# Attention stages: where the exponential, its maximum and the transposes' copy run

## The reference

```python
def _L1_attn_ref(x, w_qkv, b_qkv, w_out, b_out):
    ...
    q, k = _rope(q, k)
    scores = jnp.einsum('bhtd,bhsd->bhts', q, k) / jnp.sqrt(jnp.float32(Dh))
    scores = jnp.where(causal, scores, -jnp.inf)
    probs = jax.nn.softmax(scores, axis=-1)
    out = jnp.einsum('bhts,bhsd->bhtd', probs, v)
    ...
x = _layernorm(x + _L1_attn_ref(x, ...), axis=-1)
```

| stage | time in the span, us | scores from | mask | output projection |
|---|---|---|---|---|
| L1_attn | 5119 to 5480 | x, with rotary embedding | causal | yes |
| L1_xattn | 5480 to 5800 | x and the context | one per batch element | yes |
| L2_xattn ("recalled") | 6534 to 6790 | x and one remembered key and value for all heads | none | yes |
| L3_self | 7110 to 7430 | x, gain and shift in its norm | causal | no |
| L3_cross | 7430 to 7700 | Y and the context, gain and shift | none | no |

## Time and profile before

### The profile page before, as it was taken

How to read it: one execution, slowest core, us unless ns; L and a number is a source line. 1 busy time by engine, 2 the same in 40 slices (tenths; PEclk the granted TensorE clock), 3 DMA queues, 4 the chain that set the end, 5 groups by cost and what they waited for, 6 DMA issues and landing times. The chain is left out here.

```text
span 8333.2 us, 92849 instructions
## 1 busy us (share of the span) xinstructions
PE 6721.0 (81%) x34116; PEld 4705.7 (56%) x34116; DVE 3959.2 (48%) x8807; ACT 1842.1 (22%) x2726; POOL 1376.6 (17%) x1101
## 2 busy tenths in 40 slices
PE   5889888888888888898599998876476766778698
PEld 3666665666666566666456665554243543555454
DVE  7454455654445565444300003545487344554444
ACT  2222122222222222221121211222211233223111
POOL 2221122222212222221200001312000100222100
PEclk8776677676666767766799999877655777778899
DMA  0000000000000000000000000000000000000000
GB/s 26 1 1 1 1 1 1 1 1 1 1 1 1 1 1 1 1 1 14 35 11 21 21 11 6 0 25 13 2 1 8 20 4 4 3 17 6 4 17 23
DMA packets 13607, 64.63 MB, mean 8 GB/s; under 512 B 1168, under 2 KB 5648, under 8 KB 11152
## 3 DMA queue, kind: packets, MB, share of 16 engines
q1 hardware_dynamic: 13200, 59.09, 2.0%
HBM read 56.99 MB, written 2.10 MB: 7 GB/s over the span
## 5 line engine op out<-in xcount | busy, mean ns | idle before, releaser
L806 PE MATMUL psum<-arena,weights 32*32 32x64 f32 x8192 | 860.4, 287 | 0.0
L773 PE MATMUL psum<-arena 128*128 128x256 f32 x2048 | 596.8, 443 | 319.3 <-DVE arena L979 312.6
L806 PEld LDWEIGHTS psum<-arena,weights 32*32 32x32 f32 x8192 | 763.5, 152 | 5.8
L1219 PE MATMUL psum<-arena 128*128 128x512 f32 x1600 | 711.7, 599 | 59.5 <-DVE Y L1283 35.8
L773 PEld LDWEIGHTS psum<-arena 128*128 128x128 f32 x2048 | 448.3, 224 | 526.1 <-issue 349.5
L796 PEld LDWEIGHTS psum<-arena 32*32 32x32 f32 (+2 forms) x6144 | 591.0, 157 | 256.6 <-issue 253.9
L796 PE MATMUL psum<-arena 32*32 32x64 f32 (+2 forms) x6144 | 670.3, 293 | 0.0
L1231 PE MATMUL psum<-arena 128*128 128x256 f32 x2624 | 583.0, 380 | 4.1 <-DVE arena L1324 4.1
L1300 DVE SCALAR_TENSOR_TENSOR Y<-psum,arena,Y 128x256 f32<-128x256 f32 x416 | 172.5, 478 | 849.0 <-PE psum L1231 849.0
L1231 PEld LDWEIGHTS psum<-arena 128*128 128x128 f32 x2624 | 499.1, 190 | 111.7 <-issue 43.5
L144 POOL TENSOR_TENSOR arena<-arena,eps 128x4 f32<-128x4 f32 (+2 forms) x76 | 15.1, 199 | 3221.9 <-DVE arena L139 3221.9
(11 more groups left out here) (418 smaller groups left out, 10541.0 us busy)
## 6 DMA issues: line engine op xcount, KB each, us to landing
arena<-in_experts_L_ffn SPq DMA_DIRECT2D x8, 2052.0 KB, 8.2
arena<-in_ctxT SPq DMA_DIRECT2D x16, 512.0 KB, 3.5
arena<-in_experts_L_ffn SPq DMA_DIRECT2D x18, 384.0 KB, 3.0
weights<-in_w_L_ffn SPq DMA_DIRECT2D x1, 3072.0 KB, 9.8
weights<-in_w_L_attn SPq DMA_DIRECT2D x1, 3024.5 KB, 13.1
weights<-in_w_L_ffn SPq DMA_DIRECT2D x1, 2753.0 KB, 12.8
weights<-in_w_L_relu SPq DMA_DIRECT2D x1, 2436.0 KB, 9.4
X<-in_x SPq DMA_DIRECT2D x1, 2048.0 KB, 8.3
```

Of the source, the lines that this page charges most:

```text
L773: mm = nc.tensor.matmul(ps[:, 2 + 2 * hh + m // 2, (m % 2) * 2 * P:(m % 2 + 1) * 2 * P], kz[:, p % 2, hh, m, :], kq[:, p % 2, m, :, :], st ...
L806: mm = nc.tensor.matmul(ps[rows, 4 + h, m * DK:(m + 1) * DK], Tt[rows, h * M + m, :], rhs, start=True, stop=True)
L1219: mm = nc.tensor.matmul(ps[:, bank, :], W[s][name][:, c, f * P:(f + 1) * P], xT[:, g, c, :], start=(c == 0), stop=(c == C - 1))
```

## The change

In `attention_stage` alone:

- The scale 1/4 moves into the constant `w.heads`, so the scores come out of TensorE already scaled. With a mask VectorE only adds it.
- VectorE takes the maximum with its sign turned (`negate=True`) and no longer subtracts; the semaphore `maxima_ready` stands for `shifted`.
- ScalarE computes the exponential head by head: 8 activations of 128x128 per unit, each with its head's negated maximum as a bias per partition. It reads `pr` with a mask and PSUM without.
- The copy of the transposes to `pT` goes from ScalarE to VectorE, where it stands behind the passes of the next unit and ahead of the normalisation.
- Without a mask, TensorE's scores wait for the exponentials (`probs_ready`) of the unit whose PSUM they overwrite, as does VectorE's maximum for its `mx` buffer; ScalarE waits for the transposes of the unit whose `pr` it overwrites.

```diff
...
@@ -396,7 +396,7 @@
                         if not recalled:
                             pe.wait_ge(v_ready, (g + 1) * 2)
                     if j >= 2:
-                        pe.wait_ge(shifted, g * UNITS + j - 1)
+                        pe.wait_ge(maxima_ready if mask else probs_ready, g * UNITS + j - 1)
                     out = s_psum(j)
                     for b in range(2):
                         mm = nc.tensor.matmul(out[:, b * 4:b * 4 + 4, :], qT[:, c, u * P:(u + 1) * P],
@@ -485,13 +486,15 @@
 
             def units(g, more):
                 for j in STEPS:
-                    if 1 <= j <= UNITS:
-                        act.wait_ge(probs_turned, g * UNITS + j)
-                        nc.scalar.copy(pT[:, (j - 1) % 2, :, :], pt_psum).then_inc(probsT_ready, 1)
                     if j < UNITS:
-                        act.wait_ge(shifted, g * UNITS + j + 1)
-                        nc.scalar.activation(pr[:, j % 2, :, :], pr[:, j % 2, :, :], ACT.Exp,
-                                             scale=1.0 if mask else DH ** -0.5).then_inc(probs_ready, 1)
+                        act.wait_ge(maxima_ready, g * UNITS + j + 1)
+                        if j >= 2 and not mask:
+                            act.wait_ge(probs_turned, g * UNITS + j - 1)
+                        frm = pr[:, j % 2, :, :] if mask else s_psum(j)
+                        for h in range(HH):
+                            a = nc.scalar.activation(pr[:, j % 2, h, :], frm[:, h, :], ACT.Exp,
+                                                     bias=mx[:, j % 2, h:h + 1])
+                        a.then_inc(probs_ready, 1)
                     if more and j == UNITS + 1:
                         copy_x(g + 1)
                     if out_proj and j >= 3 and j % 2 == 1 and (j - 3) // 2 < TILES:
@@ -532,21 +535,25 @@
                     if j < UNITS:
                         n = g * UNITS + j
                         dve.wait_ge(scores_ready, n + 1)
-                        if j >= 2:
-                            dve.wait_ge(probs_turned, n - 1)
-                        s = s_psum(j)
+                        scores = s_psum(j)
                         if mask:
+                            if j >= 2:
+                                dve.wait_ge(probs_turned, n - 1)
                             if mask == "batch":
                                 if j == 0:
                                     dve.wait_ge(mask_loaded, (g + 1) * 16)
                                 m = mk[:, j // C, :]
                             else:
                                 m = w.causal
-                            chain(dve.scalar_tensor_tensor(out=pr[:, j % 2, :, :], in0=s, scalar=DH ** -0.5,
-                                                           in1=bc(m, 1, HH), op0=ALU.mult, op1=ALU.add))
-                            s = pr[:, j % 2, :, :]
-                        chain(dve.tensor_reduce(mx[:, j % 2, :], s, AX.X, ALU.max))
-                        dve.tensor_tensor(pr[:, j % 2, :, :], s, bc(mx[:, j % 2, :], 2, P), ALU.subtract).then_inc(shifted, 1)
+                            chain(dve.tensor_tensor(pr[:, j % 2, :, :], scores, bc(m, 1, HH), ALU.add))
+                            scores = pr[:, j % 2, :, :]
+                        elif j >= 2:
+                            dve.wait_ge(probs_ready, n - 1)
+                        dve.tensor_reduce(mx[:, j % 2, :], scores, AX.X, ALU.max, negate=True
+                                          ).then_inc(maxima_ready, 1)
+                    if 1 <= j <= UNITS:
+                        dve.wait_ge(probs_turned, g * UNITS + j)
+                        dve.tensor_copy(pT[:, (j - 1) % 2, :, :], pt_psum).then_inc(probsT_ready, 1)
                     if j >= 2 and j % 2 == 0 and (j - 2) // 2 < TILES:
                         u = (j - 2) // 2
                         dve.wait_ge(o_ready, g * TILES + u + 1)
@@ -569,7 +576,7 @@
                 norm.apply(dve, chain, g)
                 chain.end()
 
-            per = UNITS * (2 if mask else 1) + TILES * (1 if out_proj else 2) + norm.chained()
+            per = UNITS * (1 if mask else 0) + TILES * (1 if out_proj else 2) + norm.chained()
             norm.open(dve)
             evacuate(0)
             with dve.Fori(0, TURNS - 1) as g:
@@ -2547,7 +2554,7 @@
 
 
 def heads_mask():
-    return (np.arange(P)[:, None] // DH == np.arange(HH)[None, :]).astype(np.float32)
+    return (np.arange(P)[:, None] // DH == np.arange(HH)[None, :]).astype(np.float32) * DH ** -0.5
 
 
 def causal_mask(value):
```

More of the change, by code:

```diff
@@ L225, in attention_stage @@
     rotated, keys_spread = sem("rotated"), sem("keys_spread")
-    scores_ready, shifted, probs_ready = sem("scores_ready"), sem("shifted"), sem("probs_ready")
+    scores_ready, maxima_ready, probs_ready = sem("scores_ready"), sem("maxima_ready"), sem("probs_ready")
     probs_turned, probsT_ready, o_ready = sem("probs_turned"), sem("probsT_ready"), sem("o_ready")
@@ L275, in _ @@
                     if mask == "batch":
-                        sp.wait_ge(shifted, g * UNITS)
+                        sp.wait_ge(maxima_ready, g * UNITS)
                         sp.dma_start(mk[:, :, :], k.maskb[g]).then_inc(mask_loaded, 16)
@@ L2350, in wide_attention_stage @@
     ones_set, qk_projected, qk_ready = sem("ones_set"), sem("qk_projected"), sem("qk_ready")
-    v_projected, v_ready, scores_ready, shifted = sem("v_projected"), sem("v_ready"), sem("scores_ready"), sem("shifted")
+    v_projected, v_ready, scores_ready, shifted = sem("v_projected"), sem("v_ready"), sem("scores_ready"), sem("maxima_ready")
     probs_ready, probs_turned, probsT_ready = sem("probs_ready"), sem("probs_turned"), sem("probsT_ready")
```

## The result

| | before | after |
|---|---|---|
| median | 8334.35 us (4 runs, 8328.73 to 8337.47) | 8386.35 us (4 runs, 8375.25 to 8402.25) |
| ratio | | 1.0067, 95% interval 1.005 to 1.0085 |
| TensorE's mean granted clock, profiled execution | 0.756 | 0.751 |

A forecast was written before the change was run, and what follows sets the result against it. The prediction took the attention stages to be bound by order, no engine being full. Turn starts, pairs and ends summed to 43 us, clock falls added 7: +50, so 8387 us, own range 8355 to 8410, 8 in 10 within 8330 to 8430.

The forecast's parts named there:

- the sum: Five attention stages: starts, pairs and ends of all turns add 43 us, further clock falls 7; together +50.
- The copy behind the passes: Middle pairs: the even unit's values wait for VectorE's copy behind the next unit's passes, 0.6 us more a pair.
- The exponentials hidden in the pairs: Pairs: eight exponentials, 2.3 us from PSUM or 2.6 from SBUF, run beside copy and values (2.97) and stay hidden.
- The ends at the lower clock: Turn ends at 1.2 GHz: seventh unit's values enter the path; +1.5 L1, +2.5 L3_self, +2.25 L3_cross, +1.65 L2_xattn.
- The clock between the ends: L2_xattn and L3_cross: longer TensorE waits bring one more clock fall in half of eight turns, 4 x 1.8 = 7 us.
- The rival of the clock: Clock falls in all 16 middle pairs (29 us), stays down longer in L3_self (about 10): 8419 us; chance 0.10.
- The prediction's case against it: Against the clock deciding: in L3_cross the clock held through a 1.74 us wait, which becomes only 0.6 longer.
- The starts and L1's first pairs: Stretched subtractions vanish: masked starts -0.7 us, unmasked 0; L1's first pairs -0.7 (1.3 saved, 0.6 added).
- the overlap of the exponentials: Eight exponentials overlap at 0.27 us each from PSUM, 0.31 from SBUF; rival without overlap: 29 us more, 8416, chance 0.07.
- The copy did not hide: Faster rival: at 1.2 GHz TensorE reaches the values as the copy ends, the 0.6 vanishes everywhere: 8314 us, chance 0.12.
- the even case: Turn ends get 2.4 GHz back and no other fall comes, sum 12 us: 8349 us; chance 0.16.

The follow-up runs named there:

- The copy back: The changed kernel with only the copy of the transposes given back to ScalarE, ahead of the eight exponentials; ratio 0.9947 to the kernel before.
- the copy ahead of the passes: The changed kernel with VectorE's copy moved ahead of the next unit's passes instead of behind them; ratio 1.0213 to the kernel before.
- the wide exponential: The changed kernel with one 128x1024 exponential per unit in place of eight, the maximum not subtracted; ratio 1.0008 to the kernel before.

## Why the prediction was right

8387 was forecast and 8386.35 measured, and the mechanism is the one forecast: the even unit's values wait for a copy that stands behind the next unit's passes. That the two numbers lie within 1 us is luck: the four runs spread over 27 us, the profiled one lost 60 us in the stages where the sum has 50, and the sum's terms met less well than the total. Per turn, mean over the turns of a stage, measured (forecast), from the starts of scores and reciprocals in both traces:

| stage | start | first pair | second pair | end |
|---|---|---|---|---|
| L1, 8 turns | -1.5 (-0.7) | -1.3 (-0.7) | +2.3 (+0.6) | +1.5 (+1.5) |
| L3_self, 4 | -1.8 (-0.7) | +1.7 (+0.6) | +1.7 (+0.6) | +2.5 (+2.5) |
| L3_cross, 4 | -0.1 (0) | +1.0 (+0.6) | +1.3 (+0.6) | +2.5 (+2.25) |
| L2_xattn, 4 | -0.5 (0) | +0.6 (+0.6) | +1.5 (+0.6) | +1.9 (+1.65) |

- The copy behind the passes, 0.6 a pair: right. Where no fall differs, the first pairs of L2_xattn and L3_cross stand at +0.57 to +0.66. The copy back takes it away, the copy ahead of the passes replaces it by something worse.
- The exponentials hidden in the pairs: right, by the wide exponential. Their cost, 2.44 and 2.16 us, was below the 2.6 and 2.3 taken. For the masked ones the estimate of 2.45 from the Trainium skill ("ScalarE: Activation LUTs", section "What ACT_TABLE_LOAD costs") was nearer; for those from PSUM that estimate is too high.
- The ends at the lower clock: right to 0.3 us in every stage.
- The clock between the ends: the term itself, four more falls in L2_xattn and L3_cross for 7 us, came out. Four of their 16 middle pairs are about 2.3 us longer, and what these pairs lost above 0.6 each is 8 us. What was mis-sized stood in the sum with nothing above the 0.6: L1's second pairs, 1.6 to 2.1 above it in each turn, 14 us, and L3_self's pairs, 9 us. In L1 I took a fall as paid already: TensorE's wait was 2.68 us ahead of the transposes and is 3.23 ahead of the values, and the slow stretch behind it, before only transposes and part of the scores (2.43 us), takes in values, transposes and part of the scores (2.84).
- The rival of the clock had its 10 us in L3_self right and not its 29: by the granted clock 8 of the 16 middle pairs held a fall before the change already, and 12 hold one now. The prediction's case against it, that the clock held through 1.74 us, rests on one pair. In the turn before that of the earlier trace rows, the same pair of the kernel before waited 1.74 us too and fell:

```profile
7527.60 1.25 PE L422 MATMUL psum<-ident,arena 128*128 128x128 f32 x8 [1.74 <-ACT arena L493]
7528.64 3.46 PE L402 MATMUL psum<-arena 128*128 128x512 f32 x4
```

- The starts and L1's first pairs were mis-sized the other way: with the unstretched pass some falls went as well (a start of L1 gained 0.1 to 2.4; three of L1's eight first pairs gained 2.3 or 2.4 in place of 0.7), 18 us more gain than forecast. The two errors cancel but for some 6 us; the total was better than its parts.
- From a turn's last reciprocal to the next turn's scores the sum had nothing. In L2_xattn this grew from 10.7 to 12.0 us, 4 us in its three places, so that by the windows L2_xattn lost most (18.0 us) and not, as the prediction had it, L3_cross (17.4). Why it grew is not shown.
- The other rivals: the overlap of the exponentials is there (0.27 to 0.31 us a head). The copy did not hide: the values wait for it, 2.62 and 3.23 us in the pairs shown. Against the even case: the ends stayed at 1.2 GHz (3.59 and 3.60 us for the values).

## What to carry to other kernels

Before a copy is moved to an engine with time to spare, ask behind what it will stand there, and who waits for it: an engine's share of busy time says nothing of its order. Work that runs under another engine's wait is free only while its input comes early; handed to the stream that causes the wait, it moves from under the wait to behind it. Splitting a wide operation cost little here once the next engine could start on the parts.

## What the runs showed of the hardware

- A pair's time mostly takes a few fixed values: equal steps in the same place differ by nothing or by about 1.67 us, according to whether TensorE's clock went down behind its wait. It did behind the waits of 2.62 and 3.23 us shown above, and not behind the 1.74 of the earlier trace rows and 1.82. The wait's length alone does not settle it: L3_cross's first pairs of before, with a wait of 1.74 us in each, took 12.26 us in two turns and 10.57 in another.
- TensorE work that computes nothing shortened two stages by 34 us: the mean granted clock of L3_cross's window rose with it from 0.82 to 0.91, that of L3_self's from 0.79 to 0.84.
- A subtraction of two SBUF tiles stretched from 1.22 to as much as 2.53 us in the kernel before, while GpSimd worked on SBUF tiles. Of the 96 masked ones, the 20 that lay beside a GpSimd operation are the 20 that stretched, and each ended 1.08 us behind its end. An add of PSUM and SBUF, a maximum from SBUF and a copy from PSUM stayed within 1.23 us beside GpSimd. What GpSimd's part in it is was not tried alone.
